# Attention and FFN on one core: q and k stored once and repeated by the loads, the last FFN batch in two token halves

## The reference

```python
q = jnp.einsum('btc,hcd->bhtd', x, Wq) + bq[None, :, None, :]
k = jnp.einsum('btc,hcd->bhtd', x, Wk) + bk[None, :, None, :]
v = jnp.einsum('btc,hcd->bhtd', x, Wv) + bv[None, :, None, :]
scores = jnp.einsum('bhtd,bhsd->bhts', q, k) * scale
probs = jax.nn.softmax(scores + causal, axis=-1)
y = jnp.einsum('bhts,bhsd->bhtd', probs, v)
x = _layernorm(x + y.transpose(0, 2, 1, 3).reshape(Bn, Tn, H * D) @ Wo + bo)
fuse = silu(matmul(x, gate_w, gate_scale)) * matmul(x, up_w, up_scale)
x = _layernorm(x + matmul(fuse, down_w, down_scale))
```

## Time and profile before

| | us |
|---|---|
| median of 3 runs | 554.45 (554.3 to 556.21) |
| profiled execution, its own time | 557.38 |
| its span, first to last instruction | 555.7 |
| TensorE busy | 527.9 (95%) |
| VectorE busy | 459.4 (83%) |
| ScalarE busy | 316.1 (57%) |
| GpSimd busy | 227.3 (41%) |
| DMA | 68.19 MB in 61548 packets, mean 123 GB/s |

### The profile page before, as it was taken

The page is one execution under the profiler, slowest core; times in us unless marked ns, Lnnn a source line. Parts: engine busy times, 40 slices in busy tenths (PEclk is TensorE's granted clock), DMA queues, the critical chain, the costliest instruction groups (busy, mean ns, idle before and its releaser), DMA issues.

```text
span 555.7 us, 10699 instructions
## 1 busy us (share of the span) xinstructions
PE 527.9 (95%) x3915; PEld 355.3 (64%) x3917; DVE 459.4 (83%) x808; ACT 316.1 (57%) x579; POOL 227.3 (41%) x251
## 2 busy tenths in 40 slices
PE   8979989999999999999999999998799999999992
PEld 3644546566565655666566565563478888888892
DVE  7876768898898888889888888998748888988876
ACT  3136676667676676766766657667354454436540
POOL 5003343263254334335325434423334654456542
PEclk9988999999999999999999999999899999999998
DMA  5864876657648547456554754700000101111012
GB/s 182 268 149 145 205 231 199 142 186 220 171 156 211 178 144 203 132 164 184 161 148 158 206 155 136 156 4 2 1 0 1 40 0 39 39 38 35 5 38 76
DMA packets 61548, 68.19 MB, mean 123 GB/s; under 512 B 6328, under 2 KB 55864, under 8 KB 61496
## 3 DMA queue, kind: packets, MB, share of 16 engines
q1 hardware_dynamic: 60664, 66.59, 41.9%
q10 hardware_dynamic: 832, 0.92, 0.5%
HBM read 37.62 MB, written 29.61 MB: 121 GB/s over the span
## 4 chain that ended last, share of the span: by engine, by line
PE 78%; DMA 7%; DVE 6%; issue 4%; SPq 2%; ACT 2%; POOL 1%; POOLq 0%; DVEq 0%; ACTq 0%
PE ps L1036 16%; PE ps L989 11%; PE ps L997 10%; PE ps L878 9%; PE ps L1156 7%; PE ps L970 6%; PE ps L947 5%; PE ps L971 4%; PE ps L886 4%; DMA m_scratch<-mrow 2%; PE ps L919 2%; DMA k_scratch<-part 2%; DMA q_st<-zero_rows 2%; PE ps L930 1%; DVE nmax L633 1%
## 5 line engine op out<-in xcount | busy, mean ns | idle before, releaser
L633 DVE TENSOR_REDUCE nmax<-ps 128x2 f32<-128x1024 f32 (+1 forms) x192 | 196.6, 1040 | 49.9 <-PE ps L971 49.3
L461 ACT ACTIVATE probs<-ps 128x512 f32<-128x512 f32 x320 | 184.1, 597 | 76.8 <-PE ps L989 75.3
L385 POOL TENSOR_SCALAR_AFFINE_SELECT probs<-probs 128x512 f32<-128x512 f32 x128 | 87.1, 694 | 209.1 <-ACT probs L461 209.1
L989 PE MATMUL ps<-q_st,k_st 98*128 98x384 bf16 (+3 forms) x512 | 122.7, 303 | 4.4 <-ACT probs L461 3.7
L412 POOL TENSOR_TENSOR f_l<-f_full,f_h 128x512 fp32r<-128x512 f32 x48 | 63.7, 1328 | 72.2 <-ACT f_h L544 72.1
L970 PE MATMUL ps<-k_st,q_st 98*128 98x256 bf16 (+2 forms) x384 | 82.3, 275 | 5.7 <-DMA k_st<-k_scratch 3.2
L971 PE MATMUL ps<-k_st,q_st 124*128 124x128 bf16 x512 | 84.3, 221 | 0.0
L997 PE MATMUL ps<-probs,v_st 128*32 128x512 f32 (+3 forms) x1024 | 82.5, 438 | 0.0
L989 PEld LDWEIGHTS ps<-q_st,k_st 98*128 98x128 bf16 x512 | 44.2, 99 | 48.9 <-issue 26.8
L539 ACT ACTIVATE sgate<-ps,s_gate 128x512 f32<-128x512 f32 x48 | 32.8, 686 | 60.5 <-PE ps L1036 60.5
L971 PEld LDWEIGHTS ps<-k_st,q_st 124*128 124x128 bf16 x512 | 46.0, 98 | 18.2 <-DVE nmax L633 13.7
(11 more groups left out here) (96 smaller groups left out, 823.8 us busy)
## 6 DMA issues: line engine op xcount, KB each, us to landing
q_st<-q_scratch SPq DMA_DIRECT2D x31, 384.0 KB
k_st<-k_scratch SPq DMA_DIRECT2D x31, 384.0 KB
q_scratch<-part SPq DMA_DIRECT2D x16, 384.0 KB, 2.6
k_scratch<-part SPq DMA_DIRECT2D x16, 384.0 KB, 2.8
xT<-in_attn_xT SPq DMA_DIRECT2D x8, 512.0 KB, 3.7
q_scratch<-part SPq DMA_DIRECT2D x16, 256.0 KB, 2.9
resid<-in_attn_x SPq DMA_DIRECT2D x8, 512.0 KB, 5.9
k_scratch<-part SPq DMA_DIRECT2D x15, 256.0 KB, 2.1
```

Of the source, the lines that this page charges most:

```text
L385: pool.affine_select(out=blocks, in_=blocks, compare_op=ALU.is_ge, fill=0.0, base=0, pattern=[*pattern, [1, P]], channel_multiplier=-1).th ...
L461: act.activation(probs[:, u, :], ps[:, u % 2, :], ACT.Exp, scale=SCALE).then_inc(exp_done, 1)
L633: dve.tensor_reduce(nmax[:, i, heads[0]:heads[-1] + 1], src, AX.X, ALU.max, negate=True).then_inc(max_taken, 1)
L989: m = pe.matmul(ps[:, u % 2, c0:c0 + T - P * j], k_st[0:RP, g, h, P * j:P * j + P], q_st[0:RP, g, h, P * j:T], start=True, stop=True)
```

## The change

*Scratch layout.* `q_scratch` and `k_scratch` become tensors of 2 x 3 x 16 x 8 x 512: half of the heads, part, channel, head of the half, token. Each part is stored once. The weights and biases of q and k are permuted on the host so that the partitions of `part[:, k]` run over channel first and head second. `store_parts` has two stores: high and mid together, then low.

*Loads.* `load_rows` fills the 96 rows of a stack by parts, in three DMAs a side. For q: high three times (48 rows), mid twice (32 rows), both with a source of stride zero in its leading dimension, low once (16 rows). For k: parts 0, 1, 2 (48 rows), 0, 1 (32 rows), 0 (16 rows). A row is 4 heads of 512 tokens, 4 KB that are contiguous on both sides. With the zero rows a stack has 7 DMAs instead of 3. `part_stored` counts 32 instead of 48 a batch, `stack_loaded` 112 instead of 48. `load_stack` waits for q's stores, issues q's loads, and then does the same for k.

*Head.* Both part tensors of the first heads are stored by SyncE. The k loads of stack 0 (in halves) and of stack 1 are issued by ScalarE, after its work on the parts; SyncE issues the q loads of both.

*FFN, last batch.* Its tokens go in two halves: chunks j = 0 to 5 on tokens 0 to 255, j = 6 to 11 on the others, all at 256 columns (`WIDTH`, `chunk`). The first half takes the places of the old chunks around `down` of the batch before. Then TensorE runs j = 6, 7, 8, the down product of the first two token blocks, j = 9, 10, 11, and `last_down` for the other two blocks. `sum_out`, `out_stats`, `out_moments`, `take_rstd2` and `norm_out` are done for each half.

```diff
-    q_scratch = nc.dram_tensor("q_scratch", (H * D, NP, T), BF16, kind="Internal").ap()
+    q_scratch = nc.dram_tensor("q_scratch", (2, 3, D, H // 2, T), BF16, kind="Internal").ap()
...
+        WIDTH = [T] * (B - 1) + [T // 2]
+        def chunk(n, j):
+            return j % IC, slice(T // 2 * (j // IC), T // 2 * (j // IC) + T // 2) if n == B - 1 else slice(0, T)
...
+        Q_PARTS = ((0, 0, 0), (1, 1), (2,))
+        K_PARTS = ((0, 1, 2), (0, 1), (0,))
+        def load_rows(eng, stack, scratch, parts, g, heads, loaded):
+            row = RM
+            for run in parts:
+                src = scratch[g // 2, run[0]:run[-1] + 1, :, HG * (g % 2) + heads.start:HG * (g % 2) + heads.stop, :]
+                if run[0] == run[-1]:
+                    src = src.to_broadcast([len(run), D, heads.stop - heads.start, T])
+                eng.dma_start(stack[row:row + D * len(run), g, heads], src).then_inc(loaded, 16)
+                row += D * len(run)
...
-                if k % 2 == 0:
-                    sp.dma_start(dst[:, 0:3, :], part[:, k, 0:1, :].to_broadcast([P, 3, T])).then_inc(part_stored[k], 16)
-                    sp.dma_start(dst[:, 3:5, :], part[:, k, 1:2, :].to_broadcast([P, 2, T])).then_inc(part_stored[k], 16)
-                    sp.wait_ge(lo_ready[k], n + 1)
-                    sp.dma_start(dst[:, 5:6, :], part[:, k, 2:3, :]).then_inc(part_stored[k], 16)
...
+                sp.dma_start(dst[0:2].rearrange("a d h t -> (d h) a t"), part[:, k, 0:2, :]).then_inc(part_stored[k], 16)
+                sp.wait_ge(lo_ready[k], n + 1)
+                sp.dma_start(dst[2].rearrange("d h t -> (d h) t"), part[:, k, 2, :]).then_inc(part_stored[k], 16)
...
-                sp.dma_start(q_st[RM:RP, g], q_scratch[rows].rearrange("(h d) a t -> (d a) h t", d=D)).then_inc(stack_loaded[g], 16)
-                sp.dma_start(k_st[RM:RP, g], k_scratch[rows].rearrange("(h d) a t -> (d a) h t", d=D)).then_inc(stack_loaded[g], 16)
+                sp.wait_ge(part_stored[2 * t], (n + 1) * 32)
+                load_rows(sp, q_st, q_scratch, Q_PARTS, g, slice(0, HG), stack_loaded[g])
+                sp.wait_ge(part_stored[2 * t + 1], (n + 1) * 32)
+                load_rows(sp, k_st, k_scratch, K_PARTS, g, slice(0, HG), stack_loaded[g])
...
             store_parts(0, 0)
+            store_parts(0, 1)
+            sp.wait_ge(mask_filled, 2)
+            sp.wait_ge(part_stored[0], 32)
             for v in range(2):
+                load_rows(sp, q_st, q_scratch, Q_PARTS, 0, slice(2 * v, 2 * v + 2), half_loaded[v])
+            load_rows(sp, q_st, q_scratch, Q_PARTS, 1, slice(0, HG), stack_loaded[1])
...
+            act.wait_ge(mask_filled, 3)
+            act.wait_ge(part_stored[1], 32)
+            for v in range(2):
+                load_rows(act, k_st, k_scratch, K_PARTS, 0, slice(2 * v, 2 * v + 2), half_loaded[v])
+            load_rows(act, k_st, k_scratch, K_PARTS, 1, slice(0, HG), stack_loaded[1])
...
+            for j in range(IC, IC + 3):
+                gate_up(B - 1, j)
+            down(B - 1, (B - 1) % 2, False)
+            for j in range(IC + 3, 2 * IC):
+                gate_up(B - 1, j)
+            last_down()
```

More of the change, by code:

```diff
@@ L434, in hi_part @@
                 bias = (b_q if k % 2 == 0 else b_k)[:, k // 2:k // 2 + 1]
-                wait(act, part_stored[k], n * 48)
+                wait(act, part_stored[k], n * 32)
                 act.wait_ge(qk_full, n * 4 + k + 1)
@@ L534, in _, with silu, f_hi @@
             attention_over(act)
-            def silu(n, ic):
-                act.wait_ge(gu_full, n * IC + ic + 1)
-                wait(act, f_ready, n * IC + ic - 2)
-                act.activation(sgate[:, ic % 3, :], ps[:, GATE[ic % 3], :], ACT.Silu, scale=s_gate[:, ic:ic + 1]).then_inc(sg_ready, 1)
-            def f_hi(n, par, ic):
-                act.wait_ge(f_ready, n * IC + ic + 1)
+            def silu(n, j):
+                ic, _ = chunk(n, j)
+                act.wait_ge(gu_full, n * IC + j + 1)
+                wait(act, f_ready, n * IC + j - 2)
+                act.activation(sgate[:, j % 3, 0:WIDTH[n]], ps[:, GATE[j % 3], 0:WIDTH[n]], ACT.Silu,
+                               scale=s_gate[:, ic:ic + 1]).then_inc(sg_ready, 1)
+            def f_hi(n, j):
+                ic, cols = chunk(n, j)
+                act.wait_ge(f_ready, n * IC + j + 1)
                 wait(act, down_full, (n - 1) * 2)
-                act.activation(f_h[:, par, ic, :], f_full[:, ic % 3, :], ACT.Copy).then_inc(fhi_ready, 1)
+                act.activation(f_h[:, n % 2, ic, cols], f_full[:, j % 3, 0:WIDTH[n]], ACT.Copy).then_inc(fhi_ready, 1)
             for n in range(B):
-                for ic in range(IC):
+                for ic in range(IC if n + 1 < B else 2 * IC):
                     if n == 0 and ic == 3:
@@ new lines, in last_down @@
+            def last_down():
+                n = B - 1
+                pe.wait_ge(f_ready, n * IC + IC + 4)
+                pe.wait_ge(down_out, n * 2)
+                for ic in range(IC):
+                    pe.wait_ge(flo_ready, n * IC + IC + ic + 1)
+                    for tb in (2, 3):
+                        for f in (f_h, f_l):
+                            m = pe.matmul(ps[:, LAST[tb - 2], 0:C], f[:, n % 2, ic, P * tb:P * tb + P], w_down[:, ic, :],
+                                          start=ic == 0 and f is f_h, stop=ic == IC - 1 and f is f_l)
+                m.then_inc(down_full, 1)
@@ L1182, in _ @@
             transpose_y(W - 1)
-            gate_up(0, 0, 2)
+            gate_up(0, 2)
             transpose_yn(B - 1, 1)
-            gate_up(0, 0, 3)
+            gate_up(0, 3)
             project_o(B - 1, 0)
-            gate_up(0, 0, 4)
+            gate_up(0, 4)
             project_o(B - 1, 1)
-            gate_up(0, 0, 5)
+            gate_up(0, 5)
             pe.wait_ge(yT_out, W)
             pe.wait_ge(o_out, B * 2)
-            for n in range(B):
-                par, nxt, nxt2 = n % 2, n + 1 < B, n + 2 < B
-                if nxt:
-                    for ic in range(3):
-                        gate_up(n + 1, 1 - par, ic)
-                down(n, par, nxt)
-                if nxt:
-                    gate_up(n + 1, 1 - par, 3)
+            for n in range(B - 1):
+                par, nxt2 = n % 2, n + 2 < B
+                for ic in range(3):
+                    gate_up(n + 1, ic)
+                down(n, par, True)
+                gate_up(n + 1, 3)
@@ L1200, in _ @@
                 if nxt2:
                     make_hT(n + 2)
-                if nxt:
-                    gate_up(n + 1, 1 - par, 4)
-                    gate_up(n + 1, 1 - par, 5)
+                gate_up(n + 1, 4)
+                gate_up(n + 1, 5)
+            for j in range(IC, IC + 3):
+                gate_up(B - 1, j)
[3 more added lines that the diff above has]
+            last_down()
 def kernel(**inputs):
```

200 lines of the change are left out of this document (89 added, 111 removed).

## The result

The changed kernel took 679.5 us (median of 4 runs, 676.3 to 684.8) against 554.6 of the kernel before: a ratio of 1.226, 95% interval 1.217 to 1.235. The forecast was 591.3 us, its range ended at 630, and rival 2 stood at 716. The direction was right, the size wrong by 88 us.

What follows compares the result with a forecast made beforehand. The prediction took TensorE to bound the kernel (78% of the chain, DMA 7%), with slacks of 7.5 and 5.0 us for loads. Median 554.45 + 29.4 (steady batches) + 9.1 (first batch) - 1.6 (end) = 591.3 us; range 546 to 630.

Steps and rivals of the forecast that it cites:

- rival 2: Loads of k in parts don't fold and also run on three and two engines: 716 us, chance 0.14.
- The engines: Stack loads: q's 48- and 32-row loads run on three and two engines, k's fold and keep sixteen.
- rival 1: The repeated q loads spread over all sixteen engines, steady batches stay at 46.0 us: 546.5 us, chance 0.20.
- The row's price: Stack loads: a 4 KB row costs a busy engine 0.166 us.
- SyncE's time: Issues per stack go from 3 to 7, about 1.6 to 3.8 us, just covered by the queue's idle time.
- The end: FFN's last batch: 7.7 us after the last f_l instead of 11.5, sum -1.6 us.
- The landing of a stack: Attention loop: 2.0 us to first data plus 6.7 for the busiest engine's rows; slack 7.5 us.
- The binding wait: Steady batches: row of maxima late behind two stacks, +1.6 and +3.3 us a half, +29.4 over six batches.
- The clock after a gap: Low clock after the first batch's 3.0 us gap: half of the 3.4 us lost regained if loads spread.
- The first batch: No slack covers longer loads: stack 0 +3.1 us, a store of maxima +6, together +9.1.
- The gap at 35 us: First batch: fewer stored bytes (up to -3 us) and narrow q loads (up to +4) meet; taken as 0.
- Rival 3: Loads confined, but the stall stays inside the 7.5 and 5.0 us of slack: 555 us, chance 0.06.

## Why the prediction was wrong in size

**What held.** *The engines.* By the count of the prediction, 7037 packets under 512 B less 512 for biases and scales and 1984 for rows of maxima leave 4541 completion writes, and 200 x 16 + 60 x 2 + 66 x 16 (the k loads of 48 and 32 rows) + 33 x 3 + 33 x 2 (the q loads of 48 and 32 rows) = 4541 exactly. With the channel outermost, 7928 - 2496 = 5432 = 4541 - 165 + 66 x 16, again exactly. So q was confined to three and two engines by the source's leading dimension alone, and k folded: rival 1's and rival 2's conditions are both refuted. The rule of the Trainium skill, "DMA: Bandwidth & Descriptors", section "Rules for kernel authors", which the trace of before bore out for a dimension on both sides, holds here for one in the source alone.

*The row's price* held as a slope. In the stretch where three engines work alone they move 70 to 78 GB/s in a share of 0.19 to 0.20: 22 to 24 GB/s each, or 0.17 to 0.19 us for 4 KB against my 0.166.

*SyncE's time* held: 3.9 us a stack, where I said 3.8, and it ends at 317.8, long before the next row of maxima. *The end* held: 8 us instead of 11.5, 7.8 in the kernel with that edit alone, -1.4 us against -1.6.

**What failed.** *The landing of a stack*, "2.0 + 6.7", 8.7 us against a slack of 7.5. Measured 12.6 to 13.1 in the loop. The runs divide the 3.9 us and more: 1.8 are there on a quiet chip (10.5), by the line above the late start of a confined load; 1.1 more come in the loop even with one stack in the queues (11.6); 1.0 comes from the stack queued behind (1.3 by the averages over the loop). For the last two the windows offer a reason, which no run separates from others: while loads on all sixteen engines run beside the confined ones, a busy engine moves as little as 8 GB/s (86 GB/s in a share of 0.67, 315 to 316 us), against 22 to 24 alone. I had taken one rate for both.

*The binding wait.* I charged the delay to the row of maxima behind two stacks (+1.6 and +3.3 a half). In the changed kernel the stack itself is late by 3.8 to 7.9 us and stops TensorE first; the row of maxima then has that much more time, and waits 4.0 us in all. The stall at the stack was in my own numbers, 8.7 against 7.5, and I left it out because the other wait seemed longer. A slack of 7.5 and a landing that is wrong by 4 gives a stall wrong by 4, twice a batch: 11.4 us a batch by late rows, where the whole sum had 4.9.

*The clock after a gap*: no term at all for the steady loop. The earlier trace rows show a 3 us gap followed by 7 us at 0.51, and I used that for the first batch in rival 1 alone. The steady loop has fourteen gaps, 5.7 us on average, and TensorE's busy time rose by 34.2 us. When the gaps were filled with matmuls, 11 to 13 us came back.

*The first batch*, +9.1 forecast and +26.1 measured. Its longest stalls are the same error again. TensorE on the changed kernel, and the chain's wait that ends the batch (to lay beside the earlier trace rows):

```profile
45.04 0.48 PE L992 MATMUL ps<-k_st,q_st 98*128 98x384 bf16 x1 [6.91 <-DMA k_st<-k_scratch]
...
73.90 0.50 PE L992 MATMUL ps<-k_st,q_st 98*128 98x384 bf16 x1 [7.27 <-DMA q_st<-zero_rows]
```
```profile
106.98 8.35 DMA m_scratch<-mrow
```

The gap at 35 us, which I costed at nothing, ended at 38.0 before and ends at 45.0 now: +7.0. It waits for loads that SyncE issues from 31.12 (from 31.79 before), so it is again the landing: 13.9 us where it was 6.3. Here TensorE stands on k's side, which runs on all sixteen engines; in the kernel with the channel outermost and the same order of the head no wait for a load is left there. The first matmul on the second batch's stack 0 comes at 73.9 instead of 60.55, 6.3 more (I had 3.1). The rest of the batch loses another 12.8 (I had 6), most of it at two more stacks and at the store of 8.35 us.

*The sum* with the measured terms: 26.1 for the first batch, 15.95 on average for each of the six others (the batch's last group of output projections comes every 61.52 us on average and came every 45.56: 95.7 in six), -1.4 at the end: on the profiled span 555.7 + 26.1 + 95.7 - 1.4 = 676.1, and it was 675.8. *Rival 3* (absorbed) was wrong for the same reason as the forecast, further off.

My range ended at 630 because I had bounded the sum by half the stalls and by a row price of 0.2, and by nothing else. The start of a confined load and the low clock had no bound of their own, and these were the terms that failed.

## What to carry to other kernels

Look at the outermost dimension of a DMA's access pattern before its bytes: a repeat of 3 or 2 put there turned 554.6 into 679.5 us, and the same repeat one dimension further in cost nothing that can be measured. When a load gets longer than its slack, price it as a landing (start, rows on the busiest engine, what shares that engine), test every wait that it feeds and not only the longest one, and add the stretch at the low clock that each gap on TensorE brings. And two waits that feed the same engine can cover each other: 25 us less at one became 28 more at the other.

## What the runs showed that I had not expected

- The time SyncE needs to issue a DMA goes by the access pattern: 0.33 us folded (L369, L378 above), 0.60 with three dimensions on sixteen engines (L376), 0.72 on three engines (L364).
- Rows of 4 KB instead of 1 KB bought nothing that the runs show: with the channel outermost a stack took 6.0 us in six DMAs, in pieces of 1 KB on both sides 5.6 in two. The number of DMAs differs too, so the two sizes aren't compared alone.
- A confined load slows a small transfer behind it while most engines stand idle: the store of 8 KB took 1.9 us before, 3.9 us in the batch shown (324.64 to 328.54, at a DMA share of 0.16 and less), 6.6 where it stood directly behind a stack, and 8.4 to 9.4 in the first batches of the changed kernel (at 106.98, 170.00 and 232.12 us).
- A granted clock at the 1.2 GHz level costs less than its busy time says where the work after it is waiting for data anyway: 34 us of busy time, 11 to 13 us when most of it was taken away.
